# A fused attention and mixture-of-experts kernel: the bias of the first eight attention steps from one chunk, finer waits, and a new job list

## The reference

```python
x = x + 0.5 * ffn(layernorm(x))
x = x + attention(layernorm(x))     # 16 heads of 8, rotary, ALiBi bias, softmax over all 1024 keys, projection
x = x + 0.5 * ffn(layernorm(x))     # the same weights

def ffn(x):
    scores = sigmoid(x @ gate.T)                          # 8 experts in 2 groups, best group, best 2 of it
    routed = sum over chosen e of share_e * (relu(lat @ w1[e].T)**2 @ w2[e].T)   # lat = x @ fc1.T
    return routed @ fc2.T + relu(x @ up.T)**2 @ down.T
```

## Time and profile before

| | us |
|---|---|
| median of 3 runs | 792.69 (790.34 to 797.41) |
| profiled execution | 797.02, its span 795.2 |
| TensorE busy | 746.6 (94%), in 5542 matmuls |
| ScalarE busy | 611.5 (77%), of it 465.8 in 248 exponentials |
| VectorE busy | 431.4 (54%) |
| GpSimd busy | 199.8 (25%) |
| granted TensorE clock, mean | 0.976 |

### The profile page before, as it was taken

How to read it: one execution, slowest core, us unless ns; L and a number is a source line. 1 busy time by engine, 2 the same in 40 slices (tenths; PEclk the granted TensorE clock), 3 DMA queues, 4 the chain that set the end, 5 groups by cost and what they waited for, 6 DMA issues and landing times. The chain is left out here.

```text
span 795.2 us, 14485 instructions
## 1 busy us (share of the span) xinstructions
PE 746.6 (94%) x5542; PEld 377.8 (48%) x5542; DVE 431.4 (54%) x1160; ACT 611.5 (77%) x497; POOL 199.8 (25%) x173
## 2 busy tenths in 40 slices
PE   5998899999999999999999999999999999999977
PEld 3885443444445344344344444345444444434566
DVE  4685645626554665566644546545355464345554
ACT  3694688788788878878878898788888888887523
POOL 1014232232231232222322142131222313122230
PEclk9995799999999999999999999999999999999999
DMA  7024312022073220142231100133230020010101
GB/s 247 1 54 139 101 41 68 19 80 72 7 182 80 61 83 4 29 120 53 56 110 25 57 5 19 41 92 86 58 88 19 5 57 8 5 58 8 47 1 31
DMA packets 40941, 46.08 MB, mean 58 GB/s; under 512 B 9122, under 2 KB 27146, under 8 KB 40738
## 3 DMA queue, kind: packets, MB, share of 16 engines
q1 hardware_dynamic: 39058, 43.70, 20.2%
q10 hardware_dynamic: 1808, 1.39, 0.6%
HBM read 25.48 MB, written 19.32 MB: 56 GB/s over the span
## 5 line engine op out<-in xcount | busy, mean ns | idle before, releaser
L1322 ACT ACTIVATE weights<-f_scores 128x2048 f32<-128x2048 f32 x248 | 465.8, 1878 | 100.4 <-PE f_scores L946 94.9
L965 PE MATMUL f_acc<-weights,v_res 128*9 128x512 f32 x2048 | 268.4, 596 | 0.6 <-DVE f_o_out L1686 0.6
L1088 PEld LDWEIGHTS f_bank_o<-w_out,f_hid 128*128 128x128 f32 x928 | 120.5, 195 | 104.7 <-issue 100.0
L946 PE MATMUL f_scores<-q_op,k_full 25*128 25x512 f32 (+7 forms) x1408 | 132.6, 411 | 21.2 <-ACT weights L1322 14.7
L1088 PE MATMUL f_bank_o<-w_out,f_hid 128*128 128x128 f32 x928 | 144.1, 293 | 0.1
L1695 DVE TENSOR_TENSOR weights<-weights,ediag 128x512 f32<-128x512 f32 x128 | 89.8, 702 | 88.5 <-ACT weights L1322 84.9
L1359 POOL TENSOR_TENSOR f_hid<-f_hid,f_relu 128x512 f32<-128x512 f32 x52 | 75.2, 1446 | 140.0 <-DVE f_hid L1568 139.9
L1359 POOL TENSOR_TENSOR f_hid<-f_relu 128x512 f32<-128x512 f32 x52 | 56.1, 1080 | 210.1 <-ACT f_relu L1236 210.1
L946 PEld LDWEIGHTS f_scores<-q_op,k_full 25*128 25x128 f32 (+1 forms) x1408 | 60.9, 184 | 92.8 <-ACT weights L1322 70.2
L921 PE MATMUL f_bank_h<-xn_t,w_hi 128*128 128x512 f32 x224 | 84.7, 461 | 1.2 <-ACT f_relu L1236 1.1
L1236 ACT ACTIVATE f_relu<-f_bank_h 128x512 f32<-128x512 f32 x106 | 63.3, 597 | 22.7 <-PE f_bank_h L921 22.6
(11 more groups left out here) (238 smaller groups left out, 725.0 us busy)
## 6 DMA issues: line engine op xcount, KB each, us to landing
q_parts<-f_parts SPq DMA_DIRECT2D x24, 256.0 KB, 3.0
k_parts<-f_parts SPq DMA_DIRECT2D x24, 256.0 KB, 3.1
q_op<-q_parts SPq DMA_DIRECT2D x48, 96.0 KB
k_full<-k_parts SPq DMA_DIRECT2D x48, 96.0 KB
o_scratch<-f_o_out SPq DMA_DIRECT2D x124, 18.0 KB
x_ln<-in_L_attn_x_dram SPq DMA_DIRECT2D x8, 256.0 KB, 3.1
rope<-const_rope SPq DMA_DIRECT2D x1, 2048.0 KB, 10.4
x_scratch<-f_res SPq DMA_DIRECT2D x8, 256.0 KB, 2.3
```

Source lines behind the costliest of these rows:

```text
L946: last = nc.tensor.matmul(scores[:, j, lo:hi], k_full[rows, g, kt * P:(kt + 1) * P], q_op[rows, g, CHUNK * half + lo:CHUNK * half + hi], s ...
L965: last = nc.tensor.matmul(acc[BLOCK * j:BLOCK * j + VW, :], v_res[:, c // HALVES, kt, col:col + VW], weights[:, n % WEIGHTS, j, :], start= ...
L1088: last = nc.tensor.matmul(made[:, t * P:(t + 1) * P], hid[:, m, t * P:(t + 1) * P], w_out[:, m, :], start=(m == 0 and t == (2 * side if jo ...
L1322: nc.scalar.activation(weights[:, n % WEIGHTS, :, :], scores[:, :, :], ACT.Exp).then_inc(exps_done, 1)
```

## The change

Four things are edited. First, the bias of the first eight steps is made from the norms of chunk 0 alone, in four small operations of its own (`first_product`, `first_root`, `first_minus`, `fill_bias`) around a `cast_bounds` that now writes `bank_o`; the bound over both chunks is still made, for the later steps. Second, `load_half` waits only for the position rows of its group (`fills_through`), and VectorE's first diagonal of each group only for that group's factors (`ediags_through`). Third, SP issues the loads of chunk 1's keys for group 0 and of chunk 0 for group 1 behind the store of chunk 1, without waiting for the bound. Fourth, `pos` and `diag` get memory of their own, and `HEAD_STEPS`, `FILLS`, `DIAGONALS` and every row of `PLAN` have new numbers.

```diff
-        pos = weights[:, 0, 0:SEQ // CHUNK, :].rearrange("p j t -> p (j t)")
-        diag = weights[:, 0, 2, 0:2 * P].rearrange("p (a t) -> p a t", a=2)
+        pos, diag = sb("pos", [P, SEQ])[:, :], sb("diag", [P, 2, P])[:, :, :]
...
-HEAD_STEPS = 221
-FILLS = (140, 78, 177, 128, 134, 63, 118, 122)
+HEAD_STEPS = 216
+FILLS = (57, 163, 176, 116, 3, 119, 140, 129)
...
+def in_order_through(steps, wanted):
+
+    order = sorted(range(len(steps)), key=lambda i: (steps[i], i))
+    return 1 + max(order.index(i) for i in wanted)
+
+
+def fills_through(g):
+    return in_order_through(FILLS, (g, HG + g))
+
+
+def ediags_through(g):
+    return in_order_through(DIAGONALS, range(GH * g, GH * (g + 1)))
...
+        first_bound = sb("first_bound", [HEADS, 3])
...
-                sp.wait_ge(rows_filled, 2 * HG)
+                sp.wait_ge(rows_filled, fills_through(g))
...
             def first_operands(step):
                 if step == FIRST_JOB[0].at["store"][1] + 1:
                     load_half(0, 0, qk_loaded[0], qk_loaded[0])
+                if step == FIRST_JOB[1].at["store"][1] + 1:
+                    load_half(1, 0, late_keys, late_loaded)
+                    load_half(0, 1, qk_loaded[1], qk_loaded[1])
                 if step == FIRST_JOB[1].at["fill"] + 1:
                     sp.wait_ge(shift_ready, 1)
-                    load_half(1, 0, late_keys, late_loaded)
+                    load_shift_rows(sp, 0, 1, qk_loaded[1])
                     load_shift_rows(sp, 0, 0, late_loaded)
-                    load_half(0, 1, qk_loaded[1], qk_loaded[1])
-                    load_shift_rows(sp, 0, 1, qk_loaded[1])
...
                     if before.head:
-                        pe.wait_ge(norms_read, largest_through(FIRST_JOB[0], 1))
+                        pe.wait_ge(bias_step, 5)
...
-            def cast_bounds(job):
-
-                pe.wait_ge(norms_read, 2 * HEAD_JOBS)
-                pe.wait_ge(bound_step, 3)
-                nc.tensor.matmul(out_bank(job)[:, 0:HEADS], minus[:, 0:1].broadcast_to([HEADS, P]),
-                                 ident[0:HEADS, 0:HEADS], start=True, stop=True).then_inc(bounds_cast, 1)
+            def cast_bounds():
+                pe.wait_ge(bias_step, 3)
+                nc.tensor.matmul(bank_o[:, 0:HEADS], first_bound[:, 2:3].broadcast_to([HEADS, P]),
+                                 ident[0:HEADS, 0:HEADS], start=True, stop=True).then_inc(bias_step, 1)
...
-                        act.wait_ge(bias_ready, 1)
+                        act.wait_ge(bias_step, 5)
...
+            def first_root():
+                pool.wait_ge(bias_step, 1)
+                nc.gpsimd.tensor_tensor(first_bound[:, 1:2], first_bound[:, 0:1], half_power[:, 0:1],
+                                        ALU.pow).then_inc(bias_step, 1)
...
-            def fill_bias(job):
-                dve.wait_ge(bounds_cast, 1)
-                v.tensor_reduce(minus_all[:, :], out_bank(job)[:, 0:HEADS], AX.X, ALU.min).then_inc(bias_ready, 1)
+            def first_product():
+                dve.wait_ge(norms_read, largest_through(FIRST_JOB[0], 1))
+                v.tensor_tensor(first_bound[:, 0:1], norm_max[:, 0, 0:1], norm_max[:, 1, 0:1], ALU.mult).then_inc(bias_step, 1)
+
+            def first_minus():
+                dve.wait_ge(bias_step, 2)
+                v.tensor_scalar(first_bound[:, 2:3], first_bound[:, 1:2], -1.0, None, ALU.mult).then_inc(bias_step, 1)
+
+            def fill_bias():
+                dve.wait_ge(bias_step, 4)
+                v.tensor_reduce(minus_all[:, :], bank_o[:, 0:HEADS], AX.X, ALU.min).then_inc(bias_step, 1)
...
-                if n == 0:
-                    dve.wait_ge(ediag_ready, HEADS)
+                if c == 0 and kt == 0:
+                    dve.wait_ge(ediag_ready, ediags_through(g))
```

147 lines of the change are left out of this document (75 added, 72 removed).

## The result

The changed kernel takes 789.57 us (median of 20 runs, 786.69 to 792.70) against 793.08 for the kernel before (20 runs on the same chip, 789.29 to 803.75): a ratio of 0.995, 95% interval 0.9935 to 0.9965. Two later comparisons gave 0.9931 (0.9907 to 0.9954) and 0.9926 (0.9899 to 0.9953). It is faster by 0.5 to 0.7%, 4 to 6 us; forecast were 11.9. The time lies in the range, just under its upper end, and the direction was right. The size was 3.5 us here and 4.5 and 6.1 in the two later comparisons, a third to a half of the forecast.

What follows compares the result with a forecast made beforehand. TensorE, though 97% busy in attention, was taken to have room, with steps near the bare exponential-scores alternation and chains in head and tail. Terms -5.4 + 5.5 - 12.0 = -11.9 on 792.7 gave 780.8 us, range 772 to 790.

Steps and rivals of the forecast that it cites:

- the price of the bound: Head: the bound over both chunks costs 6.3 us, from the last DMA at 75.0 to the scores at 81.32.
- the price of the full steps: Attention: 64 instead of 53 steps with more fill than one hidden tile and one spread, 2.80 against 2.52 each: +3.1 us.
- the carrying over of stages read from one execution to the median: Sum: -11.9 us, read on the profiled 797.0, subtracted from 792.7, the median 4.3 under that execution.
- Head (-5.4): Up to the first exponential: scores at 75.9, exponential at 77.0 instead of 82.44, 5.4 us less; bounds 6.3 and 4.0.
- the bias under them: Head: the new bias is ready at about 75, 77.6 at the latest, under the keys' load landing at 75.9.
- 0.2 for all hand-overs: Head: the keys' load lands at 75.0 + 0.7, say 75.9 with the hand-overs.
- Attention (+5.5): The 255 steps: 13.2 us of TensorE work moves in, of which 3.1 for more full steps and 2.4 for first steps is paid.
- The 2.4 for the first steps: First eight steps: two hidden tiles and a gate at the low clock take about 5 us, half of it finds room.
- Rival 3: Attention pays all 13.2 us of the TensorE work moved in: 788.5 us; chance 0.07.
- Tail (-12): Behind the last exponential: merge 8.5 us earlier, turned input another 2.9, ffn 0.6 less, together 12.0; bounds 15 and 7.
- as assumed (2): Tail: 2 us of low clock kept in C7's ffn, since TensorE idles while the layer norm runs.
- The range's lower end: Time of 772 us, from head 6.3, attention 3.1 and tail 15, less than all together.

Runs made afterwards that it cites:

- experiment 2: Extra matmuls with unused results put into TensorE's waits, in the kernel before (12: ratio 0.9966; 31: 0.9939) and in the changed kernel (0.9929 to 0.9947).
- before_fourth: The kernel before, unchanged, in a fourth profiled execution: first exponential at 78.56, steps 8 to 254 in 641.2, span 794.4 us.
- w_before_both: The kernel before with 19 extra matmuls in the head's waits and 12 in the tail: median 788.27 us, ratio 0.9939.
- w_after_head: The changed kernel with 18 extra matmuls in TensorE's two idle stretches ahead of the first scores: median 790.70 us, ratio 0.9947.
- w_after_tail: The changed kernel with 26 extra matmuls while TensorE waits for the last layer norm: median 788.38 us, ratio 0.9929.
- experiment 1: Both kernels run again unchanged, to see what is the same in every execution: profiled spans 794.4 to 795.2 us before, 786.6 to 789.7 after.
- after_again: The changed kernel, unchanged, in a second profiled execution: first exponential at 76.95, steps 8 to 254 in 646.1, span 788.3 us.
- w_after_all: The changed kernel with extra matmuls in its head and tail waits and four each in steps 0, 1, 17 and 206: median 786.66 us, ratio 0.9892.

## Why the prediction went wrong

Three steps of the sum failed: the price of the bound, the price of the full steps, and the carrying over of stages read from one execution to the median.

**Head (-5.4).** The queues were read right: loads first, the bias under them (74.0, forecast about 75), the keys' low part at 67.6 for 67.0. In executions like the one shown the gain is 4.3; the 1.1 less is the landing of store and loads, on which I had added 0.2 for all hand-overs. The step that failed is "So the bound over both chunks costs 81.32 - 75.0 = 6.3 us". In these 6.3 us TensorE did its own work at half clock as well, two hidden tiles' and two norms' matmuls among it; with the clock up, what is left of them is some 1.1 (experiment 2). The 82.44 was not the kernel's own either: 78.56 in before_fourth, 75.79 with 19 extra matmuls. Over the profiled executions the head falls from a mean of 81.3 to 77.9, by 3.4, and with the clock up in both it gets longer, from 18.00 behind the copy of the values (w_before_both) to 18.85 (w_after_head).

**Attention (+5.5).** Two terms. The 3.1 for more full steps was too small: steps 8 to 254 without a fall of the clock take 6.7 us more. The count of 64 full steps was right (65 steps over 2.65 us, 55 in before); their price was near that of a hidden tile with half a pair, 2.77, which 22 of them have (mean 2.76 over the trace). But 12 steps of three half pairs and 6 with a whole value take 2.94 and 2.95. Of the first kind the trace of before has one step (251, 3.00 us), of the second none, and the 18 alone add 18 x 0.17 = 3.1. All full steps together have a mean of 2.84 instead of 2.79. The light ones kept theirs, 2.52. The 2.4 for the first steps was nearly nothing (+0.3): in before, too, the third step had had the low clock with a hidden tile in it. To this come falls of the clock in attention, 2.9 us in two of three executions, which no step of the prediction had; before had one only in before_fourth (4.5). The means: 660.3 for 255 steps before, 668.2 after, so +7.9. Rival 3's full price, 13.2, did not come.

**Tail (-12).** It was 11.0 to the last residual and 11.3 with the end, in every execution. The merge is at 12.3 behind the last exponential instead of 10.6, since the last `weigh` (748.52) waits for a diagonal product (747.69) that stands behind C6's scaling (747.08) on VectorE; 0.6 of these 1.7 came back in C7's ffn. w_after_tail shows 1.75 us of low clock in it, as assumed (2).

**The scale.** From 11.9 to the 8.6 of the shown pair are 3.3 us: head 1.1, attention 1.4, tail 0.8. From 8.6 to the 3.5 of the medians are 5.1: the profiled execution of before lies 3.9 above the median of 20, that of the changed kernel 1.2 below its own. So the larger part of the miss is not a stage but the choice of execution. I had carried the sum over from an execution 4.3 us above its median as if that offset lay outside the stages. Over all profiled executions, head -3.4, attention +7.9 and tail -11.3 are -6.8, the difference of the mean spans; the medians gave -6.1 beside the third and fourth execution, -4.5 and -3.5 in the other comparisons. All four profiled executions of before took 796 to 797 us; its shortest ones, 789 to 792, no profile has caught. That they are those with neither the long fall in the head nor one in attention (82.4 to 78.6, of it 1.5 ahead of the copy of the values, and 22.9 to 21.3 in before_fourth, with 636.5 in the others) would give 795.2 - 5.5 = 789.7 as span. Executions of that span exist (23 of the 132 lie at 789.4 to 790.3 with a mean clock of 0.979 to 0.981), but that their stages are these is argued, not shown. (The range's lower end is a slip as well: head 6.3, attention 3.1 and tail 15 give 792.7 - 18.2 = 774.5, and not 772; nothing hangs on it.) Of the rivals, 5 had the mechanism, the clock, but only as a delay that might follow the change; that it was already in the rows of the kernel before, and would go away without the change, was the case left out. The rows were there: 0.87 in the head, 0.53 behind it. The Trainium skill (TensorE: Matmul & The Clock Gate, section HAM oscillation — how this bites in real kernels) describes a kernel whose TensorE waits for DMA and starts each burst at the low clock. By that rule the idle stretches of the head had to be looked at first, and the trace agrees there, though the waits are not for DMA: in before_fourth TensorE was busy for 4.01 of the 6.00 us from 60 to 66, at clock 0.50. The falls behind the light steps have no such stretch ahead of them (experiment 1), and the 12.84 busy us of 13.00 at 0.50, from 66 to 79 in before, are no burst's start.

## What to carry to other kernels

Read the granted clock beside every duration before a stage is priced, and take more than one profiled execution: a stage at half clock is the price of an accident that the next execution may not have. When work is moved into a steady loop, price each kind of step that the new list makes, also those that the old trace doesn't show; what cost here is the new list of the jobs that had to make room, not the place of the one moved. Before a wait is priced as an end minus a start, ask at what clock the work between them ran: 6.3 us of wait held about 1.1 that the change could take away. TensorE work without a use, put into waits that exist anyway, was worth as much here as the change.

## What the runs showed of the hardware

The clock fell to 0.50 in attention behind two or three light steps in a row (in after_again TensorE was busy for 2.00 of 3.00 us ahead of it) and cost 1.2 to 1.5 us each time in the changed kernel, about 2.5 in w_after_all and about 4.5 in before_fourth, not in every execution. In the head it stayed at 0.50 for 27 to 31 us in three of four executions of the kernel before, through nearly gapless work from 66 to 79 (12.84 of 13.00 us), and in the fourth from 59 to 70 and again from 76 to 84. With 19 extra matmuls in the waits it was at 1.00 from 25 us to the end of the head. Apart from the clock, the time of the first copy of values lay between 57.99 and 59.48 us in four executions of before and between 56.25 and 59.64 in five that share the changed kernel's head. What exactly decides between these is left open.
